# A decoder layer on one Trainium2 core: GpSimd's four kinds of products and VectorE's scans, roots and sums in another order

## The reference

```
x = layernorm(x + attention(x))            # 16 heads of 128, decaying linear attention, gated, rms norm
x = layernorm(x + wkv(k=x, v=ctx_2048))    # along the 256 tokens, per channel
x = layernorm(x + ffn(x))                  # 512 -> 2048 -> 512, ternary weights, gelu

# wkv, rewritten without the running maximum, per channel c, w = exp(-exp(decay)):
aa[t+1] = w*aa[t] + e1[t]*v[t]      bb[t+1] = w*bb[t] + e1[t]      # two scans
y[t]    = (aa[t] + e2[t]*v[t]) / (bb[t] + e2[t])                   # numerator / denominator
```

## Time and profile before

| what | us |
|---|---|
| median of 3 runs (1429.12 to 1431.48) | 1429.16 |
| the profiled execution, its time | 1429.61 |
| its span, first to last instruction | 1427.2 |
| PE / DVE / ACT / POOL busy over the span | 1353.2 / 961.6 / 621.6 / 268.5 |
| mean granted TensorE clock | 0.986 |

### The profile page before, as it was taken

One profiled execution on the slowest core, in us unless ns is written; L12 is line 12 of the kernel. 1 busy time (PEld: TensorE's weight loads), 2 busy tenths in 40 slices (PEclk: granted clock), 3 DMA queues, 4 the chain that ended last, 5 costly groups with the idle time before them and its releaser, 6 DMA issues. The chain is left out here.

```text
span 1427.2 us, 21094 instructions
## 1 busy us (share of the span) xinstructions
PE 1353.2 (95%) x6898; PEld 1056.6 (74%) x6898; DVE 961.6 (67%) x1712; ACT 621.6 (44%) x1182; POOL 268.5 (19%) x199
## 2 busy tenths in 40 slices
PE   7999999998999999999999999999995789998897
PEld 6888888887888888888888888888883344454443
DVE  5666666655666657667666766555658788888873
ACT  5433434342434343433434343434331667767754
POOL 2210101110101011110101110101113454444430
PEclk9999999999999999999999999999997899999999
DMA  5011111110111010110101010000000001111000
GB/s 199 5 46 54 59 37 59 47 63 23 45 37 44 22 44 22 46 44 28 44 22 44 22 44 8 30 7 29 28 24 17 30 30 45 44 44 45 15 16 29
DMA packets 14435, 55.00 MB, mean 39 GB/s; under 512 B 2112, under 2 KB 2112, under 8 KB 12096
## 3 DMA queue, kind: packets, MB, share of 16 engines
q1 hardware_dynamic: 14400, 54.55, 11.2%
HBM read 50.35 MB, written 4.19 MB: 38 GB/s over the span
## 5 line engine op out<-in xcount | busy, mean ns | idle before, releaser
L333 PE MATMUL bank<-x_hi,w_hi 128*128 128x512 f32 x1024 | 413.3, 404 | 7.9 <-DVE x_lo L859 7.1
L335 PE MATMUL bank<-x_hi,w_lo 128*128 128x512 f32 x1024 | 401.1, 392 | 0.0
L334 PE MATMUL bank<-x_lo,w_hi 128*128 128x512 f32 x1024 | 400.1, 391 | 0.0
L844 DVE TENSOR_TENSOR resid<-resid,bank 128x512 f32<-128x512 f32 x256 | 173.6, 687 | 149.7 <-PE bank L384 148.7
L1252 POOL TENSOR_TENSOR sq_sum<-sq_sum,o_sq 128x512 f32<-128x512 f32 x64 | 104.8, 1637 | 872.2 <-ACT o_sq L604 872.2
L333 PEld LDWEIGHTS bank<-x_hi,w_hi 128*128 128x128 f32 x1024 | 193.1, 189 | 47.5 <-issue 9.1
L335 PEld LDWEIGHTS bank<-x_hi,w_lo 128*128 128x128 f32 x1024 | 192.9, 188 | 42.8
L334 PEld LDWEIGHTS bank<-x_lo,w_hi 128*128 128x128 f32 x1024 | 193.5, 189 | 36.7
L850 DVE SCALAR_TENSOR_TENSOR gated<-g_t,bank 128x512 f32<-128x512 f32 x64 | 44.0, 687 | 176.2 <-PE bank L364 176.2
L599 ACT ACTIVATE v_t<-bank 128x512 f32<-128x512 f32 x64 | 38.2, 596 | 185.9 <-PE bank L335 185.9
L382 PE MATMUL bank<-wo_hi,u_hi 128*128 128x512 f32 x256 | 100.8, 394 | 14.6 <-DVE u_lo L855 14.3
(11 more groups left out here) (147 smaller groups left out, 2401.6 us busy)
## 6 DMA issues: line engine op xcount, KB each, us to landing
w_raw<-w_ffn SPq DMA_DIRECT2D x32, 512.0 KB, 3.3
raw<-w_heads SPq DMA_DIRECT2D x15, 1024.0 KB, 4.9
raw<-w_heads SPq DMA_DIRECT2D x17, 256.0 KB, 2.7
x_in<-x_rows SPq DMA_DIRECT2D x8, 512.0 KB, 3.3
val<-ctx_t SPq DMA_DIRECT2D x8, 512.0 KB, 3.3
out<-y_out SPq DMA_DIRECT2D x8, 512.0 KB, 2.6
resid<-x_t SPq DMA_DIRECT2D x3, 1024.0 KB, 9.3
resid<-x_t SPq DMA_DIRECT2D x4, 256.0 KB, 5.2
```

Source lines behind the costliest of these rows:

```text
L333: mm(PJ[j % 2][:, :], a, c, start=kt == 0, stop=False)
L334: mm(PJ[j % 2][:, :], a, d, start=False, stop=False)
L335: last = mm(PJ[j % 2][:, :], b, c, start=False, stop=kt == KT - 1)
L844: tt(resid[:, 4 * g + t, :], resid[:, 4 * g + t, :], YB[t % 2][:, :], ALU.add).then_inc(y_added, 1)
```

## The change

On GpSimd a row now begins with the power of the input norm, then comes the denominator, then the products with the value (t1, the column, t2), the power of the output norm, the numerator and the fractions. The denominator gets a wait for ek2, which t2 had before it. On VectorE the reciprocal of the first half follows the result of batch b-1 at once, its second half follows the statistics, and the aa scans come after the second half and hidden piece 0. The sum over the input (`input_sum`) stands at the very end of a row, and for batch b+3 in place of b+2; before row 0 stands an extra one for batch 2. The shift of the input norm moves up to the middle of the row. PE, ACT and SP are unchanged.

```
 VectorE, row(b, s, ...)
                 if next_row:
                     bb_states(b + 1)
                 if not first:
                     summed = result(b - 1, 1, 1 - s)
                 if next_row:
-                    aa_states(b + 1)
+                    invert(b + 1, 0)
                 if not first:
                     after(summed)
                     bn(NO, 1, y_out[:, 1, :])
                     variances(NO, LN_EPS)
                 if next_row:
-                    invert(b + 1, 0)
+                    invert(b + 1, 1)
                 split_h(b, 0, 0)
                 if next_row:
-                    invert(b + 1, 1)
+                    aa_states(b + 1)
+                split_h(b, 0, 1)
+                if second_row:
+                    shift(NX, b + 2)
                 if not first:
                     shift(NO, b - 1)
-                for j in range(1, 4):
-                    split_h(b, 0, j)
-                if second_row:
-                    input_sum(b + 2)
+                split_h(b, 0, 2)
+                split_h(b, 0, 3)
                 if next_row:
                     second_stats(b + 1)
                 split_h(b, 1, 0)
                 if next_row:
                     root = second_shift(b + 1)
-                if second_row:
-                    shift(NX, b + 2)
                 split_h(b, 1, 1)
...
                 after(result(b, 0, s))
                 bn(NO, 0, y_out[:, 0, :])
+                if third_row:
+                    input_sum(b + 3)
...
+            input_sum(2)
             row(0, 0, first=True)
...
-            row(BATCH - 3, 1)
-            row(BATCH - 2, 0, second_row=False)
-            row(BATCH - 1, 1, next_row=False, second_row=False)
+            row(BATCH - 3, 1, third_row=False)
+            row(BATCH - 2, 0, second_row=False, third_row=False)
+            row(BATCH - 1, 1, next_row=False, second_row=False, third_row=False)
 GpSimd
             def denominator(b):
                 pool.wait_ge(scans_ok, 2 * KT * b + KT)
+                pool.wait_ge(ek2_ok, KT * b + KT)
...
             def row(b, first=False, next_row=True, second_row=True):
-                if next_row:
+                if second_row:
+                    root(NX, b + 2)
+                if next_row:
+                    denominator(b + 1)
                     weighted(b + 1)
-                    denominator(b + 1)
-                    numerator(b + 1)
                 if not first:
                     root(NO, b - 1)
                 if next_row:
+                    numerator(b + 1)
                     fraction(b + 1, 0)
                     fraction(b + 1, 1)
-                if second_row:
-                    root(NX, b + 2)
                 if next_row:
                     second_root(b + 1)
                 root(NH, b)
```

More of the change, by code:

```diff
@@ L1099, in result, with row @@
                 return step(stt(y_out[:, t, :], y_out[:, t, :], sc_pr[:, t:t + 1], x2[:, s, t, :], ALU.mult, ALU.add))
-            def row(b, s, first=False, next_row=True, second_row=True):
+            def row(b, s, first=False, next_row=True, second_row=True, third_row=True):
                 if next_row:
```

## The result

| | us |
|---|---|
| before, median of 4 runs (1428.08 to 1431.48) | 1429.14 |
| changed, median of 4 runs (1437.28 to 1441.95) | 1438.84 |
| ratio, with its 95% interval | 1.007 (1.0057 to 1.0083) |
| changed, the profiled execution: its time, its span | 1437.28, 1435.6 |

The change makes the kernel slower, by 0.57 to 0.83%. The forecast was 1434.6 in a range of 1427 to 1440: direction and mechanism hold, the size was put too small (5.4 us against 9.7). A second timing of the same kernel, experiment 9, gave 1442.17.

What follows compares the result with a forecast made beforehand. No engine is full; a ring of waits, mostly over DVE, bounds a row. Full rows change by -1.85 + 2.93 = +1.08 us; all rows give +4.45, with the power +5.4: 1434.6 us, range 1427 to 1440.

Steps and rivals of the forecast that it cites:

- Steps 1 to 4: From a row's bb-scan start (T0): scans run alone, gaining 4.24 us; four products stand bare after the numerator, to 23.3.
- Step 5: PE's transposes of num start at 23.4 after waiting 2 us; second statistics (S) at T0+24.5, first half gains 1.85 us.
- The sum: Whole kernel: all rows together +4.45 us, with the power +5.4 us, giving a median of 1434.6.
- Step 6: Input sum before the next bb scans ends at S+15.49, where ek1 would allow S+12.56; second half loses 2.93 us.
- Step 7: The moved two-element shifts may wait for num on POOL, to 18.0, at no cost.
- Step 8: Power of the input norm on POOL beside the second bb scan: 0.15 us in each of six rows.
- the first rival: The power holds the bb scans for its whole length, 0.7 us in six rows: +8.7 us, 1437.8; chance 0.12.
- the hidden sum: Input sum at the row's end lies in DVE's free time before the scans: -10.1 us, 1419.0; chance 0.09.
- the free result: Result operation no longer stands still behind den, 2.13 becomes 0.75 us in rows 1 to 6: 1426.3; chance 0.07.
- the slow data: The bb scans are slow by their data, not by POOL, so running them alone gains nothing: 1464; chance 0.01.

Runs made afterwards that it cites:

- experiment 9: The changed kernel itself timed once more, with nothing changed, for its own spread and a second trace: 1442.17 us, ratio 1.0082 to the kernel before.
- Experiment 5: Changed kernel without the addition of the key after the fraction, so two of GpSimd's four products after the numerator are left out: 1417.2 us, ratio 0.9913.
- experiment 4: Changed kernel with eleven extra 128x512 products on PE in each row, where it otherwise waits for num before the transposes: 1436.02 us, ratio 1.0047.
- experiment 2: Kernel before with only the input sum moved to the row's end, for batch b+3, with its shift and power as in the change: 1446.77 us, ratio 1.0124.
- experiment 3: Changed kernel with the second half of the projection of tile 0 ahead of PE's transposes of num: 1443.62 us, ratio 1.0101.
- experiment 8: Changed kernel with the aa scans ahead of low half 0 and of the second reciprocal, input sum left at the row's end: 1417.25 us, ratio 0.9919.
- experiment 1: Changed kernel with the input sum again for batch b+2 before the second statistics, its shift and power where they were before: 1426.26 us, ratio 0.9981.
- experiment 7: Changed kernel with the aa scans ahead of low half 0 and the second reciprocal, input sum back in the row between low halves 2 and 3: 1410.36 us.
- experiment 6: Changed kernel with the input sum back before the second statistics and the aa scans ahead of the second reciprocal, after low half 0: 1425.15 us, ratio 0.9968.

## Why the prediction was right, and by how much it was not

- *Steps 1 to 4*, the first half up to the last product: right to 0.16 us. Forecast from T0, and measured in row 1: first reciprocal 5.14, 5.26; end of the aa scans 15.71, 15.87; end of the numerator 17.98, 18.11; last product done 23.3, 23.45. The result operation is still held by den (2.23). t1 and t2 are done long before the scans. Experiment 5 shows that the products are on the path.
- *Step 5*, the transposes at 23.4 and S at T0+24.5: right in rows 0, 1 and 6 (24.63 in row 1, 24.62 in row 6), wrong by 1 us in rows 2 to 5 (25.45 to 25.50). This is the term that was mis-sized: it took 1.07 us from the transposes' start to S "as in row 6", and that holds only at full clock. It said that PE waits 2 us for POOL (it is 2.8) and let the wait cost nothing further. It costs 0.85 us in four rows, 3.4 us; experiment 4 gets 2.8 us back by filling the wait. The prediction's own row, row 3 of the kernel before, had such a fall in it, and there it lay under the next wait. That row's S of T0+26.35 is also 0.11 us later than that of rows 1, 2, 4 and 5 (DVE waits 0.99 us for the high half of piece 3 there, elsewhere 0.87), so the gain of the first half was put that much too high for these.
- *The sum*: the span grew 3.05 us beyond the forecast. That is the 3.4 us of the clock and 1.8 us of smaller things (0.4 of them in the tail of row 2), less 1.3 us for a start of row 0 earlier than forecast and 0.9 us for the power. Without these last two the miss would have been 5.2 us, so that the median lies inside the range is in part luck: the second timing, 1442.17, lies above it. The extra sum before row 0 was priced rightly, +1.64 us: with it row 0 starts at 1119.06 to 1120.23 in experiments 2, 3, 4, 5 and 8 (in 9 at 1122.71), against 1118.32.
- *Step 6*, the tail: forecast S+15.49, measured 15.47 in row 1. Experiments 1, 2 and 8 move the sum in three different surroundings, and it costs at the row's end each time. After row 2 there is 0.4 us more (15.92), in which DVE waits for nothing that the profile shows. There its program turns from one pass of its loop over rows to the next, so that is the likely cause, not a tested one; before, it would have lain under the wait for ek1. The prediction did not have it.
- *Step 7*, the shifts: they did wait for num, 1.79 us, and delayed nothing on the path.
- *Step 8*, the power: 0.15 us a row were taken for it; it was 0. The scans take 2.44 us with it and 2.43 alone (aa). It is the power that is held, 1.06 to 1.17 us instead of 0.70. The Trainium skill ("SBUF — State Buffer", "Who interferes with whom") lets the order of issue decide who waits: the scan was there first, and the power waited, as two-element shifts waited for num. That the power in its turn would hold the next scan for its whole length, which the first rival took from it, the trace doesn't show. In row 3 the power was even there first (1238.12, 0.70 us), and the scans from 1238.45 on took 2.44 us as elsewhere.
- The rivals: the hidden sum, the free result and the slow data are refuted by the lines above, the power that holds the scans as well. That 1437.8 for that rival comes near the result is an accident: its mechanism isn't there.

What stays open: why the clock falls in some of these waits and not in others. In experiment 1 PE waits 3.3 us in rows 0, 1, 2 and 5, and only row 0 has the long transposes; in rows 3 and 4, after 2.6 us, they take 1.35 and 1.97 us. The kernel before has waits of 2.05 us in rows 1 to 5, and only row 3 shows a fall.

## What to carry to other kernels

In a row that is a ring of waits, look at what precedes the next round's first instruction on its engine: an independent sum of 3.3 us cost 0.8 us (experiment 1) and 1.5 us (7 against 8) in the middle, where the engine had time, and 2.9 us at the end, where it waited 0.4. When an engine is freed of contention, ask which of the moved operations now stand bare between the last scan and the next engine's work. And price a new wait of TensorE with what its clock does after it; filling the wait with dummy products gave 2.8 us, while an order of the scans in which there is no such wait gave 21.6 us with the sum still at the row's end (experiment 8), and 28 us with the sum in the row (experiment 7). Before putting a miss down to the clock, look at a row in which the clock stayed up: in experiment 6 such rows are only 0.3 us shorter than the others.

## What was not expected of the hardware

- Eleven products that nobody reads make the kernel faster: after a wait of 2.8 us eight transposes took 1.92 to 1.97 us in four and in five of seven rows, at a granted clock of 0.52 (row 2), and 1.09 after a wait of 0.4.
- Even operations of two elements are held by a large one with two SBUF inputs on the other engine: VectorE's shifts 1.79 us behind the numerator, GpSimd's power took up to 1.17 us (0.70 alone) beside a scan. The copy of four elements takes 0.19 us now and took 0.59 beside the scans.
